# Folding the key weights of a head pair in two 128-row products, and the output's fold moved to the mixes' column tiles

## The reference, cut to what matters

```python
q = x @ q_a_w.T @ q_b_w.T                      # rank 192; per head 64 columns without, 64 with rotation
ckv = x @ kv_a_w.T                             # 64 shared latent columns, 64 rotated ones
kvb = (k_pass_c @ kv_b_w.T)                    # per head: 64 key columns, 128 value columns
scores = einsum('bhqd,bhkd->bhqk', query, key)
attn = softmax(scores)
out = einsum('bhqk,bhkd->bhqd', attn, v)
return out.transpose(0, 2, 1, 3).reshape(B, S, H * V_D) @ o_w.T
```

## Time and profile before

| | |
|---|---|
| median of three runs | 1535.77 us (1535.66 to 1535.92) |
| span of the profiled execution | 1532.5 us |
| busy: PE, DVE, ACT, POOL | 1472.6, 1165.9, 845.5, 634.4 us |
| attention A's loop | from about 60 to 377 us |
| one L869 to the next, slot with s=3 (query fold) | 10.94 us |
| slot with s=0 | 9.43 us |
| slot with s=1 (output fold) | 10.42 us |
| slot with s=2 | 9.63 us |

### The profile page before, as it was taken

How to read it: one execution, slowest core, us unless ns; L and a number is a source line. 1 busy time by engine, 2 the same in 40 slices (tenths; PEclk the granted TensorE clock), 3 DMA queues, 4 the chain that set the end, 5 groups by cost and what they waited for, 6 DMA issues and landing times. The chain is left out here.

```text
span 1532.5 us, 26829 instructions
## 1 busy us (share of the span) xinstructions
PE 1472.6 (96%) x9032; PEld 1272.6 (83%) x9032; DVE 1165.9 (76%) x2628; ACT 845.5 (55%) x2072; POOL 634.4 (41%) x516
## 2 busy tenths in 40 slices
PE   8799999998799999988999999999999879999998
PEld 6677777786688888876899999999999868888887
DVE  7888899999765555587888888888888777555554
ACT  4788888886433333226766666666666433333322
POOL 2588888885100000017766666666666210000000
PEclk9899999999999999998999999999999999999999
DMA  2254444545110000003223223213222200010001
GB/s 101 59 126 121 119 121 121 127 107 142 49 42 21 22 21 0 0 5 96 53 70 68 65 63 69 70 42 86 67 49 54 50 22 22 21 42 21 0 1 56
DMA packets 65976, 91.55 MB, mean 60 GB/s; under 512 B 7232, under 2 KB 60480, under 8 KB 65856
## 3 DMA queue, kind: packets, MB, share of 16 engines
q1 hardware_dynamic: 65856, 90.02, 22.7%
HBM read 29.18 MB, written 2.10 MB: 20 GB/s over the span
## 5 line engine op out<-in xcount | busy, mean ns | idle before, releaser
L1841 DVE TENSOR_TENSOR f_hidden<-ps,f_silu 128x512 f32<-128x512 f32 x128 | 87.7, 690 | 201.5 <-PE ps L122 201.5
L481 POOL TENSOR_TENSOR ab_swapped<-ab_swapped,const 128x512 f32<-128x512 f32 x126 | 162.8, 1292 | 167.3 <-ACT ab_swapped L476 167.3
L1732 ACT ACTIVATE f_silu<-ps 128x512 f32<-128x512 f32 x128 | 76.3, 598 | 277.1 <-PE ps L122 277.1
L120 PE MATMUL ps<-xh,f_wl 128*128 128x512 f32 x512 | 203.2, 397 | 1.6 <-DVE f_hidden L1841 1.6
L121 PE MATMUL ps<-xl,f_wh 128*128 128x512 f32 x512 | 202.8, 396 | 0.0
L122 PE MATMUL ps<-xh,f_wh 128*128 128x512 f32 x512 | 202.5, 396 | 0.0
L1543 POOL TENSOR_TENSOR ab_qk<-ab_qk,ab_swapped 128x512 f32<-128x512 f32 x126 | 172.5, 1369 | 9.9
L1311 ACT ACTIVATE ab_probs<-ab_probs,ab_negmax 128x128 f32<-128x128 f32 (+1 forms) x256 | 114.6, 448 | 80.5 <-DVE ab_negmax L1414 78.5
L73 POOL TENSOR_TENSOR rstd<-shifted,minus_half 128x4 f32<-128x4 f32 x16 | 16.2, 1013 | 338.2 <-DVE shifted L67 335.1
L120 PE MATMUL ps<-f_wh,f_hl 128*128 128x256 f32 x512 | 144.2, 282 | 0.4 <-DVE x L1857 0.4
L121 PE MATMUL ps<-f_wl,f_hh 128*128 128x256 f32 x512 | 143.9, 281 | 0.0
(11 more groups left out here) (212 smaller groups left out, 4442.7 us busy)
## 6 DMA issues: line engine op xcount, KB each, us to landing
ab_probsT<-ab_squares SPq DMA_DIRECT2D x128, 192.0 KB, 3.7
aa_probsT<-f_stages SPq DMA_DIRECT2D x128, 128.0 KB, 2.6
b_stages<-keys SPq DMA_DIRECT2D x128, 128.0 KB, 2.7
f_stages<-wf_in SPq DMA_DIRECT2D x16, 768.0 KB, 4.3
b_stages<-wb_qkv_in SPq DMA_DIRECT2D x8, 768.0 KB, 6.0
a_stage<-wa_in SPq DMA_DIRECT2D x8, 608.0 KB, 5.0
x<-x_in SPq DMA_DIRECT2D x4, 512.0 KB, 7.0
b_stages<-wb_out_in SPq DMA_DIRECT2D x8, 256.0 KB, 3.9
```

The source lines that it names most:

```text
L120: nc.tensor.matmul(out, ll, rh, start=start, stop=False)
L481: return engine.tensor_tensor(by_batch(out), by_batch(src), table(c, rows, col), ALU.mult)
L1841: nc.vector.tensor_tensor(hidden[:, m, :], UP(m), silu[:, m, :], ALU.mult).then_inc(hid_done, 1)
```

## The change

The staged key weights of a pair become a block-diagonal 128x128 matrix, made on the host: head 0's 64x64 in the upper left, head 1's in the lower right, zeros elsewhere. A pair's query fold is then two products over all 128 rows (L421 in the new numbering) instead of four over 64, and there is no wait between the heads. ScalarE's four casts become two of double width, VectorE's two subtractions one; in the opening VectorE's four become two. The output's fold moves on TensorE from the end of step 1 to step 2, between the scores and the mixes, and its cast and subtraction on ScalarE and VectorE from step 2 to step 3. The wait in `turn_inverse` is unchanged. The staged weights grow from 1216 to 1280 columns, and the split small weights sh and sl are now allocated for the opening alone.

```diff
@@ opening
-                fold_product(nc, SPARE[:, 0:P], stage, 0).then_inc(fold_ready, 1)
-
-                pe.wait_ge(fold_ready, 1)
-                fold_product(nc, SPARE[:, P:2 * P], stage, 1)
+                fold_product(nc, SPARE[:, 0:2 * P], stage)
...
-def fold_product(nc, bank, stage, h):
-
-    r = slice(64 * h, 64 * h + 64)
+def fold_product(nc, bank, stage):
+
     for m in range(2):
-        ins = nc.tensor.matmul(bank[:, m * KVR:(m + 1) * KVR], stage[r, A_PASS + m * P:A_PASS + (m + 1) * P], stage[r, A_K:A_K + KVR], start=True, stop=True)
+        ins = nc.tensor.matmul(bank[:, m * P:(m + 1) * P], stage[:, A_PASS + m * P:A_PASS + (m + 1) * P], stage[:, A_K:A_K + 2 * KVR], start=True, stop=True)
     return ins
...
@@ attention_a, TensorE
                 after(pe, spread_done, n)
-                fold_product(nc, FOLD(it)[:, 0:P], stage, 0).then_inc(fold_ready, 1)
-
-                pe.wait_ge(fold_ready, 2 * it - 1)
-                fold_product(nc, FOLD(it)[:, P:2 * P], stage, 1).then_inc(fold_ready, 1)
+                fold_product(nc, FOLD(it)[:, 0:2 * P], stage).then_inc(fold_ready, 1)
...
-                if j == 1 and s == 1 and it + 1 < HP:
-
-                    pe.wait_ge(spread_done, n)
-                    fold_output(it + 1, INVERSE)
                 if j == 2:
+                    if s == 1 and it + 1 < HP:
+
+                        pe.wait_ge(spread_done, n)
+                        fold_output(it + 1, INVERSE)
                     mix(n, 0)
                     mix(n, 1)
...
@@ attention_a, ScalarE
-                act.wait_ge(fold_ready, 2 * it)
-                for h in range(2):
-                    ins = fold_upper(nc, FOLD(it)[:, h * P:(h + 1) * P], stage, wh[:, it % 2], h)
-                ins.then_inc(fold_hi, 1)
+                act.wait_ge(fold_ready, it)
+                fold_upper(nc, FOLD(it)[:, 0:2 * P], stage, wh[:, it % 2]).then_inc(fold_hi, 1)
...
-                if j == 2 and s == 1 and it + 1 < HP:
+                if j == 3 and s == 1 and it + 1 < HP:
                     fold_output(it + 1, INVERSE)
...
@@ attention_a, VectorE
-                for h in range(2):
-                    (upper, source), _ = fold_parts(FOLD(it)[:, h * P:(h + 1) * P], stage, wh[:, it % 2], h)
-                    ins = nc.vector.tensor_tensor(wl[:, it % 2, :, h, 0:KVR], source, upper.bitcast(F32), ALU.subtract)
-                ins.then_inc(fold_lo, 1)
+                (upper, source), _ = fold_parts(FOLD(it)[:, 0:2 * P], stage, wh[:, it % 2])
+                nc.vector.tensor_tensor(wl[:, it % 2, :, :, 0:KVR], source, upper.bitcast(F32), ALU.subtract).then_inc(fold_lo, 1)
...
-                if j == 2 and s == 1 and not last:
+                if j == 3 and s == 1 and not last:
                     fold_output(it + 1, INVERSE)
...
@@ host
-    wk = kvb[:, :, :NOPE].reshape(HP, P, KVR)
+    wk = _np.zeros((HP, 2, NOPE, 2, KVR), _np.float32)
+    for h in range(2):
+        wk[:, h, :, h, :] = kvb[:, h, :NOPE]
+    wk = wk.reshape(HP, P, 2 * KVR)
```

More of the change, by code:

```diff
@@ L30 @@
 LOGIT_LOWER = float(np.log(GOLDEN_LOWER / (1.0 - GOLDEN_LOWER)))
-A_PASS, A_K, A_ROT, A_V, A_O = 0, 256, 320, 576, 704
-A_COLS = 1216
+A_PASS, A_K, A_ROT, A_V, A_O = 0, 256, 384, 640, 768
+A_COLS = 1280
 C_COSA, C_SINA, C_COSB, C_SINB, C_IDENT, C_MASK = 0, 256, 512, 768, 1024, 1152
@@ L132, in opening @@
         swapped = sb("swapped", [P, 2, G])
+        sh, sl = sb("sh", [P, KD, S_WR], F32R), sb("sl", [P, KD, S_WR], F32R)
         x_in = [sem(f"x_in_{s}") for s in range(NG)]
@@ L182, in project @@
                     for k in range(KD):
-                        ins = matmul3(nc, out, (c.sh[:, k, col], c.sl[:, k, col]), (c.xh[:, k, slot(s)], c.xl[:, k, slot(s)]), k == 0, k == KD - 1)
+                        ins = matmul3(nc, out, (sh[:, k, col], sl[:, k, col]), (c.xh[:, k, slot(s)], c.xl[:, k, slot(s)]), k == 0, k == KD - 1)
                     ins.then_inc(ready, 1)
@@ L244, in split_small @@
                 act.wait_ge(wr_zero, 1)
-                nc.scalar.copy(c.sh[:], small_in[:, :, 0:S_WR])
+                nc.scalar.copy(sh[:], small_in[:, :, 0:S_WR])
                 nc.scalar.copy(c.wr[:, :, 0:E], small_in[:, :, S_WR:S_WR + E]).then_inc(small_hi, 1)
@@ L249, in fold @@
                 act.wait_ge(a.wo_ready, 1)
-                for h in range(2):
-                    ins = fold_upper(nc, SPARE[:, h * P:(h + 1) * P], stage, a.wh[:, 0], h)
-                ins.then_inc(fold_hi, 1)
+                fold_upper(nc, SPARE[:, 0:2 * P], stage, a.wh[:, 0]).then_inc(fold_hi, 1)
                 nc.scalar.copy(a.woh[:, 0, :], SPARE[:, 2 * P:]).then_inc(a.wo_hi, 1)
@@ L321, in fold @@
                 dve.wait_ge(a.wo_hi, 1)
-                for h in range(2):
-                    ins = fold_lower(nc, SPARE[:, h * P:(h + 1) * P], stage, a.wh[:, 0], a.wl[:, 0], h)
-                ins.then_inc(fold_lo, 1)
+                fold_lower(nc, SPARE[:, 0:2 * P], stage, a.wh[:, 0], a.wl[:, 0]).then_inc(fold_lo, 1)
                 nc.vector.tensor_tensor(a.wol[:, 0, :], SPARE[:, 2 * P:], a.woh[:, 0, :].bitcast(F32), ALU.subtract).then_inc(a.wo_lo, 1)
@@ L421, in keys_lo_parts, with both_heads, fold_parts, fold_upper @@
     return engine.tensor_tensor(in_fours(a.kl[:, slot]), every_fourth(a.keys[:, slot]), in_fours(a.kh[:, slot].bitcast(F32)), ALU.subtract)
-def fold_product(nc, bank, stage, h):
-    r = slice(64 * h, 64 * h + 64)
+def fold_product(nc, bank, stage):
     for m in range(2):
-        ins = nc.tensor.matmul(bank[:, m * KVR:(m + 1) * KVR], stage[r, A_PASS + m * P:A_PASS + (m + 1) * P], stage[r, A_K:A_K + KVR], start=True, stop=True)
+        ins = nc.tensor.matmul(bank[:, m * P:(m + 1) * P], stage[:, A_PASS + m * P:A_PASS + (m + 1) * P], stage[:, A_K:A_K + 2 * KVR], start=True, stop=True)
     return ins
[L432 to L439, removed]
+def both_heads(columns):
+    return columns.rearrange("p (m h d) -> p m h d", m=2, h=2)
+def fold_parts(bank, stage, w):
+    return ((w[:, :, :, 0:KVR], both_heads(bank[:, 0:4 * KVR])), (w[:, :, :, KVR:P], both_heads(stage[:, A_ROT:A_ROT + 4 * ROT])))
+def fold_upper(nc, bank, stage, wh):
+    for upper, source in fold_parts(bank, stage, wh):
         ins = nc.scalar.copy(upper, source)
     return ins
-def fold_lower(nc, bank, stage, wh, wl, h):
-    for (upper, source), (lower, _) in zip(fold_parts(bank, stage, wh, h), fold_parts(bank, stage, wl, h)):
+def fold_lower(nc, bank, stage, wh, wl):
+    for (upper, source), (lower, _) in zip(fold_parts(bank, stage, wh), fold_parts(bank, stage, wl)):
         ins = nc.vector.tensor_tensor(lower, source, upper.bitcast(F32), ALU.subtract)
```

7 lines of the change are left out of this document (2 added, 5 removed).

## The result

| | before | after |
|---|---|---|
| median, in one comparison of five runs each | 1535.77 us (1534.01 to 1536.45) | 1541.28 us (1537.98 to 1542.68) |
| span of the profiled execution | 1532.5 us | 1540.3 us (its time 1542.68) |

The ratio is 1.0036, interval 1.0025 to 1.0047: slower by 5.5 us, more than the 3.1 us that the prediction took as the least that can be told from no change. The forecast was 1543.

What follows compares the result with a forecast made beforehand. Fold slots were taken to run over ScalarE and VectorE, TensorE a close second. Lateness 3.5 to 5.1, pair 0 about 0.2, casts and subtractions -1.4 gave 1538.9; clock falls +4.8 gave 1543.7, say 1543; range 1533 to 1550.

Steps and rivals of the forecast that it cites:

- The wait, its place and its size: Step 3, slots s=1: TensorE's transposition waits for VectorE's output-fold subtraction, seven times, 2.4 to 2.7 us in pairs 1 to 6.
- VectorE first: VectorE's sines precede GpSimd's addition where they meet: addition ends near 207.2, ScalarE's cast at 208.14, VectorE's subtraction at 208.59.
- What is left of it at the end of the round: After the stall the path is 0.58 to 0.85 us later, 3.5 to 5.1 us over pairs 1 to 6.
- from there TensorE is just ahead again: After the next slots' row maximum, TensorE recovers by saving 0.2 us of waits a slot and 1.05 at the next query fold.
- The clock: Attention A's loop: clock falls to 1.2 GHz behind three of seven stalls, 1.6 us each, +4.8 us.
- The query fold: Merged casts save 0.15 us and subtractions 0.06: path 0.21 shorter in six loop folds, 0.15 ahead of them, together 1.4.
- TensorE as the bound: Rival: TensorE is the bound and does not wait, so both folds gain, 1525 to 1527 us; chance 0.11 with partial forms.
- The small stall: Rival: output-fold stall of 1.8 us, path late 0 to 0.1 a pair, clock holds, 1534.5 us; chance 0.17.
- the two cases with the full stall: Stall without any clock fall, 1538 to 1540 us, chance 0.27; stall with falls in some pairs, 1541 to 1548, chance 0.37.
- the one with falls in some pairs: The forecast itself: output-fold stall in attention A with clock falls in some pairs, 1541 to 1548 us; chance 0.37.
- the decision point at 1.8 us: Slower if the output fold's subtraction ends over 1.8 us behind TensorE; up to there slack and savings pay for it.

Runs made afterwards that it cites:

- The repeated trace: The changed kernel measured once more, with a second trace and another chip's comparison: 1541.54 us beside 1536.56, ratio 1.0040.
- the filled stall: The changed kernel with ten dead products on TensorE ahead of the waiting transposition in slots s=1: 1537.12 us beside 1535.13, ratio 1.0004.
- the query fold alone: The changed kernel with the output fold's product, cast and subtraction back where they were: 1535.62 us beside 1535.13, ratio 1.0003.
- the kernel with cast and subtraction in step 2: The changed kernel with the output fold's cast and subtraction back in step 2, TensorE's product as changed: 1535.77 us beside 1535.13, ratio 1.0006.
- the kernel with the cast in step 2: The changed kernel with only ScalarE's cast of the output fold back in step 2: 1535.41 us beside 1536.56, ratio 0.9993.

## Why the prediction was right, and where it was off

**The wait, its place and its size**: right. Seven times, 2.41 to 2.42 us of idle time in six of them, the lower end of the 2.4 to 2.7, and in the variant "VectorE first" the subtraction ends 8.12 us behind L859 of the slot (211.04 less 202.92; forecast 208.59 less 200.44, 8.15). The row maximum of the next slot's step 1 is 0.6 us late; forecast 0.58. One term was added wrongly: 206.35 less 0.24 is 206.1, not 206.2, for TensorE's arrival. It did no harm, for TensorE came later than either, at 206.3 on that clock (211.18 less 2.42 is 208.76, 5.84 behind L859).

**What is left of it at the end of the round**: off, and this is the mis-sized term. The sum took 0.58 to 0.85 a pair, less the query fold's 0.21, so 0.4 to 0.6 a round. Measured was 0.1: the rounds without a fall take 40.50 to 40.52 us beside 40.42. The s=1 slot is 0.46 longer, but the s=2 slot, forecast "longer than 9.6", takes 9.46 instead of 9.63. The step that failed is "from there TensorE is just ahead again", with nothing said of VectorE and GpSimd. In step 2 of slot s=2 VectorE's sines meet GpSimd's addition. After, they begin at 218.87, 0.90 us behind it (217.97), and take 0.92 us; before, they began only 0.59 us behind it and took 1.25. The rows of before, VectorE and GpSimd:

```profile
215.79 1.25 DVE L481 TENSOR_TENSOR a_swapped<-a_swapped,const 64x512 f32<-64x512 f32 x1
```

```profile
215.20 1.29 POOL L962 TENSOR_TENSOR a_raw<-a_raw,a_swapped 64x512 f32<-64x512 f32 x1
```

In both kernels the sines end 0.54 or 0.55 us behind GpSimd's addition, at 217.04 and 219.79, whenever they began. GpSimd's addition is only 0.29 us late (14.76 us behind L869 of the s=1 slot before, 15.05 after), so half of VectorE's 0.6 is gone; why GpSimd is only that late was not followed further. The Trainium skill (SBUF — State Buffer, Who interferes with whom) says that a VectorE instruction with two inputs in SBUF and a GpSimd instruction that reads SBUF exclude each other, and that the later one is blocked until the first is through. The traces agree, here and in the slot with 1.82 us: the sines end 0.54 to 0.55 us after the addition that had begun first, a little less than the 0.69 they take alone. Seen so, the estimate could have been made ahead of the run from the earlier trace rows, where 1.24 us stand for the same meeting.

**The clock**: the mechanism right, two terms off against each other. Forecast were three falls of 1.6 us, 4.8 together. This trace has four in the loop's stalls. A round with one takes 41.63 to 41.79 us, 1.1 to 1.3 more than one without; the four cost about 4.9. So part of the 1.7 us of matmul time that a fall takes is no loss to the path, more of it than forecast. The repeated trace has two. The count of three had no row behind it: that the place where a stall starts decides is shown by no run; the runs show only that stalls of one length are followed by a fall at one time and not at another. That the falls, with the idle time ahead of them, carry most of the loss is shown by the filled stall, not only by these sums.

**The total.** By the slots, six rounds are 0.5 us longer by the stall less the query fold, the first pair 0.1, four falls add 4.9, and a fall at the end of the loop and a wait beside it add 1.9, less 0.1 in the opening: 7.3, as between the two L859 above. The prediction had no term for the fall at the end of the loop. It follows two waits of TensorE; in the trace of after:

```profile
365.40 0.39 PE L120 MATMUL ps<-kh,a_ql 128*128 128x256 f32 x1 [0.67 <-ACT aa_probs L756]
367.41 0.35 PE L120 MATMUL ps<-kh,a_ql 128*128 128x256 f32 x1 [1.03 <-POOL a_ql L960]
```

Every kernel of the study has these two waits to 0.02 us, the one before too, and the fall stands in six of the twelve traces. So the forecast's sum had the lateness 1.7 to 3.3 us too large, and in this execution one more fall at a stall and the one at the end made up for it. That the total came within 1.7 us of the median (1541.28; this execution took 1542.68) is in part luck: the mechanism was right, the two terms were off in opposite directions.

**The query fold**: the path got 0.21 us shorter, as worked out; the products took 0.36 us (184.72 to 185.08) instead of the estimated 0.45, the output fold's 0.48 (204.77 to 205.25) instead of 0.43. ScalarE's casts took 0.58, forecast 0.56:

```profile
184.72 0.61 PE L421 MATMUL ps<-a_stage 128*128 128x128 f32 x4
185.08 0.36 PE L120 MATMUL ps<-kh,a_ql 128*128 128x256 f32 x1
```

```profile
228.05 0.37 ACT L437 CAST a_wh<-ps 128x256 fp32r<-128x256 f32 x1
228.32 0.41 ACT L437 CAST a_wh<-a_stage 128x256 fp32r<-128x256 f32 x1
228.63 0.48 ACT L756 ACTIVATE aa_probs<-ps,aa_negmax 128x256 f32<-128x256 f32 x1
```

Whether the time of a whole execution gains these 1.4 us is open: with 12 runs each, the query fold alone and the kernel with cast and subtraction in step 2 were at 1.0003 and 1.0006, with lower ends 0.9993 and 0.9998.

**The rivals.** TensorE as the bound falls with the query fold alone: 1.05 us fewer matmuls a fold, and the slot shrinks by the casts' 0.2. The small stall (1.8 us) didn't come: the meeting at 207.84 held GpSimd up, ScalarE's two casts stood behind GpSimd's addition, and VectorE waited 0.76 us for the second of them; the kernel with the cast in step 2 has about that stall and came out at no change, but its s=1 slots are shorter for another reason too, so the decision point at 1.8 us was not tested by itself. Of the two cases with the full stall, the one with falls in some pairs came, and the filled stall shows the other: without falls the same lateness costs nothing that the ratio can tell.

## What to carry to other kernels

An engine that looks full by its busy time can have a path beside it: ask in which order the *other* engines come to the step, and move the steps that wait behind work that doesn't. Here a subtraction that stood 1.38 us for a cast, set behind two instructions that don't need it, shortened its slot by 0.8 us (10.73 to 9.97), where the merged products and casts had brought 0.2. Before a step is moved later, look at who writes the bank that it reads: a shared buffer turns a free shift on one engine into a stall on another, and a stall of TensorE can cost the clock as well as the time.

## What the runs showed of the hardware

- Ten dead products in a stall, in whose trace the clock stayed at its upper level in all rounds, took the ratio from 1.0036 and 1.0040 to 1.0004, some 5 us (3.5 and 3.0 by the medians), though they compute nothing. The falls in the two traces of the changed kernel account for 2.3 to 4.9 of that.
- A stall's length alone doesn't say whether the clock falls. In the two traces of the changed kernel five of twelve stalls of 2.4 us were followed by a fall, and one of the two of 2.05 to 2.08 us in the first pair. In the kernel with the cast in step 2 a stall of 2.70 us was followed by none, and the first pair's, with 1.91, by one. At the end of the loop two waits of 0.67 and 1.03 us were followed by a fall in six of twelve traces. What else decides is open.
- Which of VectorE and GpSimd comes 0.01 us first to a meeting was worth 1.1 us in the one slot where it changed: sines of 1.82 instead of 0.69 us, and a slot of 11.15 instead of 10.02. When VectorE is first, GpSimd's addition takes 1.81 instead of 1.28 us.
